# Three PSUM banks in turn for the wide products of a strip, and both outputs of a round in one bank, in a fused deformable-convolution kernel

## The reference, cut to what matters

```python
om2 = conv2d(out, w_om2, b_om2)                 # 9 y-offsets, 9 x-offsets, 9 masks for each pixel
samp = bilinear_gather(x, py, px)               # 9 samples for each pixel
samp = samp * mask[:, None]
out = jnp.einsum('bckhw,ock->bohw', samp, weight.reshape(Co, Cx, KK))
out = batchnorm(out, bn2_g, bn2_b, bn2_m, bn2_v)
out = gelu(out + identity)
```

## Time and profile before

| | |
|---|---|
| median of 3 runs | 8342.6 us (8338.94 to 8348.57) |
| the profiled execution's own time | 8339.34 us |
| its span on the core, first to last instruction | 8337.5 us |
| PE busy | 6098.2 us, 73% |
| DVE busy | 4698.9 us, 56% |
| POOL busy | 5533.2 us, 66% |
| ACT busy | 2008.5 us, 24% |
| mean granted TensorE clock | 0.817 of 2.4 GHz |

### The profile page before, as it was taken

How to read it: one execution, slowest core, us unless ns; L and a number is a source line. 1 busy time by engine, 2 the same in 40 slices (tenths; PEclk the granted TensorE clock), 3 DMA queues, 4 the chain that set the end, 5 groups by cost and what they waited for, 6 DMA issues and landing times. The chain is left out here.

```text
span 8337.5 us, 110679 instructions
## 1 busy us (share of the span) xinstructions
PE 6098.2 (73%) x38788; PEld 4405.1 (53%) x38788; DVE 4698.9 (56%) x10889; ACT 2008.5 (24%) x3025; POOL 5533.2 (66%) x5485
## 2 busy tenths in 40 slices
PE   7996777875777765777863323359998998998998
PEld 5774555553555554555642211136666666666665
DVE  5665666664666664666653222235565656556666
ACT  1111112121111121111121111113333343333443
POOL 0004777777777777777777777776667667666776
PEclk9997888886888876888875555569898998889999
DMA  4222333332333332333322221222233322322332
GB/s 123 71 71 77 92 90 91 92 90 76 88 88 90 88 88 78 92 88 86 92 82 64 57 52 51 52 64 73 74 76 81 77 74 71 85 77 66 86 77 73
DMA packets 376814, 658.97 MB, mean 79 GB/s; under 512 B 121336, under 2 KB 279352, under 8 KB 368696
## 3 DMA queue, kind: packets, MB, share of 16 engines
q0 software_dynamic: 175104, 358.96, 17.0%
q1 hardware_dynamic: 201272, 294.06, 11.4%
HBM read 610.22 MB, written 42.42 MB: 78 GB/s over the span
## 5 line engine op out<-in xcount | busy, mean ns | idle before, releaser
L708 POOL DMA_INDIRECT G<-table,IDX x5472 | 5519.1, 1009 | 2759.6 <-issue 2306.4
L1124 ACT ACTIVATE SAMP<-RED 96x384 f32<-96x384 f32 x1216 | 591.4, 486 | 5147.9 <-PE RED L877 2219.9
L1649 DVE TENSOR_TENSOR ARENA<-ARENA 128x288 f32<-128x288 f32 x3744 | 1457.4, 452 | 543.5 <-PE RED L892 525.3
L892 PE MATMUL RED<-IDENT,ARENA 128*96 128x128 f32 x11232 | 1514.4, 295 | 302.7 <-DVE ARENA L1649 302.7
L892 PEld LDWEIGHTS RED<-IDENT,ARENA 128*96 128x96 f32 x11232 | 1341.5, 137 | 460.8 <-issue 402.1
L1527 DVE TENSOR_TENSOR G<-G,W 128x1152 f32<-128x1152 f32 x540 | 734.5, 1360 | 1362.0 <-DMA G<-table,IDX 1356.5
L950 PE MATMUL BTP<-PAD,ARENA 80*128 x3456 | 1259.8, 478 | 245.1 <-DVE PAD L1520 125.3
L877 PE MATMUL RED<-IDENT,SUM 128*96 128x128 f32 x1248 | 291.4, 357 | 1472.4 <-DVE SUM L1541 1464.0
L877 PEld LDWEIGHTS RED<-IDENT,SUM 128*96 128x96 f32 x1248 | 148.8, 154 | 1590.7 <-DVE SUM L1541 1169.7
L802 PE MATMUL OFFC<-PAD,ARENA 128*54 128x256 f32 (+3 forms) x3726 | 965.1, 418 | 27.4 <-ACT PAD L1051 15.3
L950 PEld LDWEIGHTS BTP<-PAD,ARENA 80*128 80x128 f32 x3456 | 595.1, 199 | 667.4 <-issue 581.6
(11 more groups left out here) (169 smaller groups left out, 4413.0 us busy)
## 6 DMA issues: line engine op xcount, KB each, us to landing
ARENA<-wtab SPq DMA_DIRECT2D x208, 800.0 KB
G<-table,IDX POOLq DMA_INDIRECT x5472
ARENA<-xo SPq DMA_DIRECT2D x96, 720.0 KB
table<-TB SPq DMA_DIRECT2D x64, 384.0 KB, 2.8
X<-x SPq DMA_DIRECT2D x2, 3200.0 KB, 22.3
out<-X SPq DMA_DIRECT2D x20, 320.0 KB
wtab<-TB SPq DMA_DIRECT2D x16, 384.0 KB, 2.9
PAD<-x SPq DMA_DIRECT2D x4, 800.0 KB, 6.7
```

The source lines that it names most:

```text
L708: pool.indirect_dma_start(G[:, b, k, :], None, tables[seg.table], bass.IndirectOffsetOnAxis(ap=IDX[:, q, b * TAPS + k:b * TAPS + k + 1], a ...
L892: last = nc.tensor.matmul(RED[b % 2][0:TPG * C, gr * 128:(gr + 1) * 128], PROD[gr][:, sft, :], IDENT[:, :], start=(sft == 0), stop=(sft == ...
L1124: nc.scalar.activation(SAMP[:, x], RED[x][0:TPG * C, 0:GROUPS * 128].rearrange("p (g n) -> p g n", g=GROUPS), ACT.Copy).then_inc(z.samp_re ...
L1649: last = nc.vector.tensor_tensor(out=PROD[gr][:, :, j * C:(j + 1) * C].rearrange("p (dy dx) c -> p dy dx c", dy=3), in0=win[:, gr:gr + 3, ...
```

## The change

Three edits. The wide products take three banks in turn, `BTP0`, `BTP1` and `OUT1`, and product `c` waits until product `c - 3` has been read. To free `OUT1`, both outputs of C2 go into `OUT0`, 256 columns each; since DVE may not read a bank into which PE still writes, the residual of either output waits for the last projection of both (`unit(now.u, UNITS - 1, 1)`). The lone tile's projection waits for the reading of both outputs before it (`u + 2`), and `calibrate`, once before the first strip, waits until the outputs of the convolution before have been read.

```diff
+TAPB = 3
...
+        TAP = BTP + [OUT[1]]
...
+        def out_slot(seg, po):
+            return OUT[0][:, po * 256:(po + 1) * 256] if seg.z is main and seg.s == C2 else OUT[po][:, 0:256]
+
         def out_tile(seg, po):
-            return OUT[po][rows(seg.p), 0:256]
+            return out_slot(seg, po)[rows(seg.p), :]
...
-                        pe.wait_ge(z.out_read, u + 1)
+                        pe.wait_ge(z.out_read, u + 2 if z is main and seg.s == C2 else u + 1)
...
                 def calibrate(n):
+                    pe.wait_ge(main.out_read, U_C2 + 2)
...
-                        if c > 1:
-                            pe.wait_ge(weighted, c - 1)
+                        if c >= TAPB:
+                            pe.wait_ge(weighted, c + 1 - TAPB)
...
-                        nc.tensor.matmul(BTP[c % 2][:, 0:TAPW], TXB[tt][:, im, k, :],
+                        nc.tensor.matmul(TAP[c % TAPB][:, 0:TAPW], TXB[tt][:, im, k, :],
...
-                            last = nc.tensor.matmul(OUT[(now.u + kind) % 2][at:at + C, b // 2 * 128:(b // 2 + 1) * 128],
+                            last = nc.tensor.matmul(out_slot(now.g, (now.u + kind) % 2)[at:at + C, b // 2 * 128:(b // 2 + 1) * 128],
...
-                            out=PRODS[gr][:, :, j * C:(j + 1) * C], in0=BTP[c % 2][:, 0:TAPW].rearrange("p (w c) -> p w c", w=WY),
+                            out=PRODS[gr][:, :, j * C:(j + 1) * C], in0=TAP[c % TAPB][:, 0:TAPW].rearrange("p (w c) -> p w c", w=WY),
...
-                    on.add_residual(now.s if kind else now.g, now.u + kind, (now.u + kind) % 2, unit(now.u, UNITS - 1, kind))
+                    on.add_residual(now.s if kind else now.g, now.u + kind, (now.u + kind) % 2, unit(now.u, UNITS - 1, 1))
```

More of the change, by code:

```diff
@@ L853, in project_unit @@
                     if b == 0:
-                        pe.wait_ge(z.out_read, u + 1)
+                        pe.wait_ge(z.out_read, u + 2 if z is main and seg.s == C2 else u + 1)
                     at = seg.p % 2 * R2 + b % 2 * C
                     for gr in range(GROUPS):
-                        last = nc.tensor.matmul(OUT[po][at:at + C, b // 2 * 128:(b // 2 + 1) * 128], WDCN[:, seg.s, gr, :],
+                        last = nc.tensor.matmul(out_slot(seg, po)[at:at + C, b // 2 * 128:(b // 2 + 1) * 128], WDCN[:, seg.s, gr, :],
                                                 SAMP[:, x, gr, :], start=(gr == 0), stop=(gr == GROUPS - 1))
```

## The result

The changed kernel takes 8034.64 us (median of six runs), the kernel before 8352.05 beside it (median of six, 8338.94 to 8366.72). Five of the six runs lie between 8012.51 and 8040.67; the sixth took 8818.21 at a granted clock of 0.66 instead of 0.82 and is left out of the ratio. The ratio is 0.9614 [0.9596, 0.9632]: 3.9% faster.

The account below looks back on a forecast made before the run. PE, waiting for DVE's reads, was taken to bound the last third. POOL would take over: its 349 us of waits less 36, 55 and 13 gave 245, so 8339.3 - 245 = 8094, forecast 8098 us, range 8040 to 8200.

Parts of the forecast that it names:

- What bounded the kernel: Last third of the kernel: PE leads and POOL follows; PE's wide products wait 213.5 us for DVE's reads.
- The ordinary group: PE's wide products: the third starts 1.08 us after the first, not 1.45; 0.37 us a group, 4.4 a round.
- The two other terms: Unit 3's stall behind `place`, 2.0 us a round; the slow clock after it, 1.6 us without a build step.
- The clock: PE in rounds with a build step: 13.9 us slow, costing 6.9; half, 3.4 us, comes back.
- POOL takes over: Last third: rounds come to POOL's pace, 47.8 to 48.7 us a tile, so PE's 411 us gain shrinks to 245.
- A dearer gather: POOL's 1843 gathers: 1.340 us each instead of 1.310 as DVE works denser, a charge of 55 us.
- Rival 2: POOL's gathers keep 1.310 us and the builds keep up: 313 us gained, 8026 us, chance 0.04.
- The waits that stay: POOL's waits for DVE's sums: 16.5 us at the first tile, 6.4 at three pair changes, small ones; 36 us.
- Builds and tail: Rounds with a build step where PE stays behind POOL, and the last pair's tail: 13 us charged.
- Rival 1: POOL's gathers get dearer than charged, 1.40 us each: 147 us gained, 8192 us, chance 0.10.
- Rival 3: PE's clock does not recover, since PE stands about 4 us a round for POOL: 8140 us, chance 0.12.
- Rivals 4 and 5: 4: third product waits for something else, 8339 us, chance 0.03; 5: two open sums in one bank slow projections, 8389, 0.04.

Follow-up runs that it names:

- before_32: The kernel before with 32 instead of 36 gathers issued for each gathered tile of C2: 8337.57 us, ratio 0.9999 to the kernel before.
- the two edits alone: Changed kernel with two product banks, only the output bank shared: 8347.92 us, 1.0005; changed kernel with three banks but the old wait: 8344.79 us, 0.9996.
- after_32: The changed kernel with 32 instead of 36 gathers issued for each gathered tile of C2: 7893.30 us, ratio 0.9463 to the kernel before.
- after: The changed kernel itself, with all 36 gathers for a tile: 8034.64 us, ratio 0.9614 to the kernel before.
- share_only: The changed kernel with two banks again for the wide products, the outputs still sharing one bank: 8347.92 us, ratio 1.0005 to the kernel before.

## Why the prediction was right and where it failed

**What bounded the kernel: right.** `before_32` shows that POOL did not lead, the two edits alone that only the wait mattered.

**The ordinary group: right, a little too small.** The third product starts 1.08 us after the first, as worked out. But the next instruction behind it follows sooner too, since the two instructions of that product take 0.70 us and not 0.80: from the first product to the projection it was 6049.32 - 6047.14 = 2.18 us and is 5814.39 - 5812.68 = 1.71. A group gains 0.47 us, not 0.37. With 12 groups that is 5.6 us a round for 4.4. The two other terms fit: 5.6 + 2.0 + 1.6 = 9.2 us of the 9.4 by which a round without a build step fell (52.2 to 42.8). Without the clock it fits as well: the round of 50.6 us that had no fall leaves 7.8 for 5.6 + 2.0. What the prediction had wrong there is that the clock falls with every stall: it did with 41 of 47.

**The clock: I took half, nearly all came back.** A round with a build step has 3.4 us at the slow clock (0.96 in the window above) where it had 13.9. By my pricing that and the rest would be 5.6 + 2.0 + 5.2 = 12.8 us; the round fell by 10.2 (57.9 to 47.7). The groups inside the slow stretch were priced twice, and the build's transposes take 1.83 us at the end of a fast stretch where they took 1.59 in a slow one. The wait behind the build stayed 0.99 and got 0.17 ahead of it, for the +0.9 that I had charged.

**POOL takes over: right.** It is the main claim: DVE waits 279.0 us for gathers, all of it ahead of `scale`, POOL no longer waits, and PE's own gain of 411 us was not to be had. `after_32`, where PE leads, gains 448 us on the kernel before beside it; `after_32` to `after` is 141 us that POOL costs (126 by the ratios). The sum on POOL's account was the right sum: 323 us in the stretch against 323.8 us of waits gone.

**A dearer gather: the step that failed.** I charged 1843 x 0.030 = 55 us, from a rate that had been seen where POOL ran without waits. It measured 1.311 us for 1.310, so 0 us. The mean of a gather was to rise above 1025 ns and fell from 1025 to 1011. The two rates of the earlier trace rows were read as a trend with density; they were two samples of how starts fall on DVE's work, and in the last pair of the changed kernel the rate is (424.0 + 126.9) / 427 = 1.290. That pair, which I let gain next to nothing, thus gains some 24.5 us of waits and 466 x 0.031 = 14 us by cheaper gathers. Rival 2, to which I gave 0.04, is what happened as to the mean: its 8026 us are 9 from the median. That they are so near is partly luck: it kept 36 us of waits where 25 stayed, and the earlier stages took 16.5 us more. The middle pairs did get dearer (1.301 to 1.326 and 1.308 to 1.315), so nought is a sum over four pairs and not a price that stood still.

**The waits that stay: 25 us for 36.** The three waits of 6.4 us at a change of pair are gone; DVE now waits for POOL, so POOL finds its buffers free. **Builds and tail: 13 us charged, none seen.** Rounds with a build step take 47.7 us in the first pair, POOL needs 36 x 1.311 = 47.2 for a tile.

In sum 55 + 11 + 13 = 79 us were charged that did not come. That makes 245 + 79 = 324, of which the earlier stages, 16.5 us later in this execution, took back enough to leave 307. The largest of the three mis-sized terms is the dearer gather.

**The other rivals.** Rival 1 (1.40 us) was the wrong way. Rival 3: the clock is at 0.96 and 1.00 in the windows, so it recovers although PE stands 3.4 us a round in waits for POOL. Rivals 4 and 5 are out by the result and by `share_only`. The 45 us below which I would have been wrong about POOL were undercut by rounds without a build step (42.7 to 42.8); those were at the end of the first pair, where POOL had a lead to use up. A mean over a pair would have been the right test; the ten rounds from 7416.6 to 7879.1 us take 46.3 each. The 48 to 50 us forecast for rounds of either kind did not come: they take 42.7 to 49.7.

## What to carry to other kernels

When a wait is removed from the leading engine, make the sum on the account of the engine that takes over: what it waited for is what can be gained, at its present rate. Charge it a worse rate only with a mechanism, and test that on the durations in the trace, sorted by where one instruction starts in the other; two means from two stretches show no trend. Here a third buffer for the producer was worth three times a new place for the long piece in the consumer's order (317 us for 102), which only moved the stall.

## What the hardware showed that was not expected

A gather on POOL that starts 0.05 us or more after a `scale` (VectorE, two inputs in SBUF, 1.36 us) began is held and ends 0.82 us after `scale` ends: all 582 such gathers of the changed kernel, with 2.13 us as the longest. One that starts up to 0.1 us ahead of it, or less than 0.03 behind it, takes 0.94 to 0.99. Of the 27 between 0.03 and 0.05, four are held.

A matmul group that waits 0.20 us for a bank loses 0.47.

A stall of PE of 2.0 us ahead of unit 3's third product was followed by half the clock 41 times and by the full clock six times (projections of up to 1.50 us, and of 0.85).

On three of the chips the same program takes a third longer (11004 to 11227 us for 8343), from its first gather on and not before.
